# Moving the routing products of a recurrence from VectorE to GpSimd

## The chip, the cores and the metric

The kernel runs on one core of a Trainium2 chip. The metric is the device time of one execution, in microseconds (us), as the median of several runs. The engines are TensorE (PE in the profile, PEld for its weight loads), VectorE (DVE), ScalarE (ACT), GpSimd (POOL) and SyncE (SP), each with its own queue of instructions that it works off in order; they meet at semaphores.

## The reference, cut to what matters

The kernel computes a windowed attention block and then a mixture of experts, whose routing comes from a GRU. Only the GRU and the dot products made from its states matter here:

```python
xw = hidden_states @ gru_w_ih.T                  # per token, 3 * 1024 columns
def step(h, xw_t):                               # 512 steps, one after the other, batch 8
    hw = h @ gru_w_hh.T
    r = sigmoid(xr + hr); z = sigmoid(xz + hz); n = tanh(xn + r * hnn)
    h_new = (1.0 - z) * n + z * h
routing = l2norm(hs.reshape(B, S, 8, 128))       # eight vectors of 128 per token
expr = (hidden_states @ expr_w.T).reshape(B, S, 8, 128)
gram = einsum('bsed,bsfd->bsef', routing, routing)
num = sum(expr * routing); norm(expr); norm(routing)
```

The routing therefore needs, for each token and each of the eight experts e, products of length 128: the state of e with the states of e to e+4 (the Gram matrix is symmetric, so five shifts are enough), and the expression vector of e with the state and with itself.

## The kernel before, in words

The recurrence runs 512 steps in 32 tiles of 16 steps. A tile is 128 tokens (16 steps by batch 8), and its body is eight pairs of steps; the first pair of a tile is written out apart, the other seven are a loop. The steps of a pair are q = 0 and q = 1. Each step has two halves of the state, A (half 0) and B (half 1).

The cycle of one step is this. TensorE waits for `h_ready` of half B, does the last 32 matmuls that half A of the next step needs (L868), and signals `gates_psA`; it then does 48 more for half B (`gates_psB`), and 48 further matmuls that need only half A of the new state. VectorE turns the sums out of PSUM (L946, L947), adds their parts (L928), and with ScalarE's sigmoid (L1012) and tanh (L1015) and GpSimd's `keep` and `not_z` (L855, L856) makes the new half of the state: `fresh` (L968), the first fp16 part (L970), the fp32 state (L971), and the second fp16 part (L973), which signals `h_ready`. It does so for half A, then for half B.

Behind half B VectorE has work that belongs to the routing of the tile before, whose states ScalarE has copied into `routes` in the first pair of the present tile (L733, L736; `tile_read`). Pair i treats expert i:

- in step q = 0: the five state products, 128x640 (L746), and their sums along 128 (L751) into `gram`;
- in step q = 1: the turn of the next tokens' share (L934, L937), then the two expression products, 128x256 (L742), and their sums (L751).

Products and sums share one buffer, `products`. All of it is in program order on VectorE: the turn of half A of the next step (L946) stands behind the sums. `dots_half` and `dots_done` say that a pair's first and second sums are made.

Of the kernel before, what the change touches and what calls it, by code (L numbers as in the profile page):

```python
# [18 lines left out]
def sandwich(nc, x, qkv_w, qkv_b, rpb, proj_w, proj_b, w_ih, w_hh, expr_w, ctx_w, ctx_b,  # L19
# [27 lines left out]
    with ctx:  # L47
# [634 lines left out]
        x_tile = sb("x_tile", [P, P])  # L682
        routes = sb("routes", [P, 2, WRAP, P])
        products = sb("products", [P, NSHIFT, P])
        gram = sb("gram", [P, NT + 1, NEXP, NSHIFT + 2])
        xn_ps = sem("xn_ps")
        xn_read = sem("xn_read")
# [19 lines left out]
        tile_ps = sem("tile_ps")  # L707
        tile_read = sem("tile_read")
        tile_staged = sem("tile_staged")
        multiplied = sem("multiplied")  # L710
        dots_half = sem("dots_half")
        dots_done = sem("dots_done")

# [22 lines left out]
                last = nc.scalar.copy(routes[:, 1, 4 * h:4 * h + 4, :].rearrange("p e d -> p (e d)"), psum[:, 6 + h, :])  # L736
            return last

        def expr_dots(e):

            here = routes[:, :, bass.ds(e, 1), :].rearrange("p a e d -> p a (e d)")
            return nc.vector.tensor_tensor(products[:, 0:2, :], here, routes[:, 1, bass.ds(e, 1), :].to_broadcast([P, 2, P]), ALU.mult)  # L742

        def state_dots(e):

            return nc.vector.tensor_tensor(products[:, :, :], routes[:, 0, bass.ds(e, 1), :].to_broadcast([P, NSHIFT, P]),  # L746
                                           routes[:, 0, bass.ds(e, NSHIFT), :], ALU.mult)

        def sum_dots(slot, e, lo, n):
            dst = gram[:, bass.ds(slot, 1), bass.ds(e, 1), lo:lo + n].rearrange("p a e s -> p (a e s)")  # L750
            return nc.vector.tensor_reduce(dst, products[:, 0:n, :], axis=AX_X, op=ALU.add)  # L751

        def tokens(i):

# [5 lines left out]
        with nc.Block() as block:  # L760
# [17 lines left out]
            @block.vector  # L778
            def _(dve):
                nc.vector.tensor_reduce(x_mean[:, :], xn2T[:, :].rearrange("p (t b) -> p b t", b=B), axis=AX_X, op=ALU.add)  # L780
                dve.drain()
                nc.vector.tensor_scalar(x_mean[:, :], x_mean[:, :], 1.0 / L, None, ALU.mult).then_inc(mean_done, 1)
                dve.wait_ge(h0_ps, 1)
                dve.wait_ge(cleared, 1)
                full = by_chunk(h_full[:, 0, :])
                nc.vector.tensor_tensor(full, by_chunk(psum[:, 0, 0:CH * B]),
                                        ctx_bias[:, :].unsqueeze(2).to_broadcast([P, CH, B]), ALU.add)
                dve.drain()
                nc.vector.tensor_reduce(w_top[:, :], h_full[:, 0, :], axis=AX_X, op=ALU.max,
                                        apply_absolute_value=True).then_inc(h0_top, 1)  # L790


                dve.wait_ge(h0_all, 1)
                nc.vector.tensor_scalar(h_all[:, :], h_all[:, :], 1.0, None, ALU.max)
                dve.drain()
                nc.vector.tensor_scalar(h_exp[:, :], h_all[:, :].bitcast(U32), 0x7F800000, None, ALU.bitwise_and)
                dve.drain()
                nc.vector.tensor_scalar(h_scale[:, :], h_exp[:, :], -1.0, float(266 << 23), ALU.mult, ALU.add)
                nc.vector.tensor_scalar(h_unscale[:, :], h_exp[:, :], float(12 << 23), None, ALU.subtract)
                dve.drain().then_inc(h_scaled, 1)  # L800
                nc.vector.tensor_scalar(neg_h_scale[:, :], h_scale_f, -1.0, None, ALU.mult)
                nc.vector.tensor_tensor(unscale[:, :], w_unscale[:, :].bitcast(F32), h_unscale_f, ALU.mult)
                nc.vector.tensor_scalar(h_full[:, 0, :], h_full[:, 0, :], h_scale_f[:, 0:1], None, ALU.mult)
                dve.drain()
                nc.vector.tensor_copy(part(h_parts[:, 0, :, :], 0), full)
                dve.drain()
                nc.vector.tensor_tensor(part(h_parts[:, 0, :, :], 1), full, part(h_parts[:, 0, :, :], 0), ALU.subtract)
                for i in range(4):

                    dve.wait_ge(x_first, i + 1)  # L810
                    nc.vector.scalar_tensor_tensor(token_part(i, 1), tokens(i), h_scale_f[:, 0:1], token_part(i, 0),
                                                   ALU.mult, ALU.subtract)
                dve.drain()


                for half in range(2):
                    dve.sem_inc(h_ready[half], 1)
                    dve.sem_inc(bank_free[half], 1)
                dve.sem_inc(kept, 2)
                dve.sem_inc(tile_staged, 1)  # L820
                dve.sem_inc(tile_read, 1)
                dve.sem_inc(dots_done, 1)

            @block.tensor
# [6 lines left out]
        with nc.Block() as block:  # L831
# [12 lines left out]
            def _(pool):  # L844
                nc.gpsimd.tensor_copy(x_now[:, :], x_parts[:, 0:2, :].rearrange("p t k -> p (t k)")).then_inc(x_staged, 1)

                def pair(n, i, first):
# [4 lines left out]
                    for q in range(2):  # L852
                        for half in range(2):
                            pool.wait_ge(rz_done[half], t0 + q + 1)
                            nc.gpsimd.tensor_tensor(keep[:, half, :], rz[:, half, 1, :], h_full[:, q, half * HB:(half + 1) * HB], ALU.mult)  # L855
                            nc.gpsimd.tensor_scalar(not_z[:, half, :], rz[:, half, 1, :], neg_h_scale[:, 0:1], h_scale_f[:, 0:1], ALU.mult, ALU.add).then_inc(keep_done[half], 1)  # L856
                    if first:
                        nc.gpsimd.tensor_copy(x_tile[:, :], xn2T[:, bass.ds(n * P, P)]).then_inc(tile_staged, 1)

# [64 lines left out]
            def _(dve):  # L924
# [50 lines left out]
                def pair(n, i, first):  # L975
                    t0 = n * SP_T + 2 * i
                    for q in range(2):
# [7 lines left out]


                        if q == 0:
                            dve.wait_ge(tile_read, n + 2)
                            state_dots(i).then_inc(multiplied, 1)
                            dve.wait_ge(multiplied, t0 + 1)  # L990
                            sum_dots(n, i, 0, NSHIFT).then_inc(dots_half, 1)
                        else:
                            turn_xn(n * PAIRS + i + 2)
                            dve.wait_ge(dots_half, n * PAIRS + i + 1)
                            expr_dots(i).then_inc(multiplied, 1)
                            dve.wait_ge(xn_ready, n * PAIRS + i + 2)
                            dve.wait_ge(multiplied, t0 + 2)
                            sum_dots(n, i, NSHIFT, 2).then_inc(dots_done, 1)

                turn_xn(1)  # L1000
                dve.wait_ge(xn_ready, 1)
# [3 lines left out]
            def _(act):  # L1005
                def pair(n, i, first):
                    t0 = n * SP_T + 2 * i
                    for q in range(2):
                        t1 = t0 + q + 1
                        for half in range(2):  # L1010
# [10 lines left out]
                                       h_parts[:, 1 - q, :, 2 * (1 - q) * B:2 * (2 - q) * B].rearrange("p c (s b) -> p c s b", b=B)  # L1021
                                       ).then_inc(kept, 1)
                        if first and q == 0:
                            act.wait_ge(dots_done, n * PAIRS + 1)
                            tile_copies(act).then_inc(tile_read, 1)

# [18 lines left out]
        with nc.Block() as block:  # L1045
# [35 lines left out]
            def _(dve):  # L1081
                dve.wait_ge(last_read, 1)
                for e in range(NEXP):
                    expr_dots(e)
                    dve.drain()
                    sum_dots(NT, e, NSHIFT, 2)
                    dve.drain()
                    state_dots(e)
                    dve.drain()
                    sum_dots(NT, e, 0, NSHIFT)  # L1090
                    dve.drain()


# [316 lines left out]
```

## Time and profile before

| what | value |
|---|---|
| median of 3 runs | 4774.18 us (4764.96 to 4792.71) |
| span of the profiled execution | 4784.5 us (no other time of that execution is given) |
| TensorE busy | 3953.2 us, 83% |
| VectorE busy | 3284.3 us, 69% |
| ScalarE busy | 1204.3 us, 25% |
| GpSimd busy | 768.7 us, 16% |
| mean granted TensorE clock | 0.97 |

The recurrence fills the span from about 580 to 4330 us. Busy shares are means over the span; what sets the time of a step is read from the order of events inside one pair. A row of the timeline gives the start, the duration, the engine, the line, what is written and read, and in square brackets how long the engine was idle just before and what ended that.

### The profile page before, as it was taken

What the parts mean: (1) busy time and instruction counts of PE and PEld (TensorE: products, weight loads), DVE (VectorE), ACT (ScalarE), POOL (GpSimd) and SP (SyncE); (2) the same over time, 40 slices, a digit from 0 to 9 for tenths busy, and PEclk for the clock granted to TensorE, in tenths of its full rate; (3) what the DMA queues carried; (4) which work ended last, traced back from release to release, by engine and by line L of the source; (5) the groups of instructions that cost most, each with busy time, mean ns of one, the idle gap of its engine ahead of it and who ended that gap; (6) DMA issues with size and microseconds to landing.
All of it is one profiled execution on the core that took longest, in us unless ns stands there. A gap on an engine that the chain in (4) does not pass through costs nothing. (4 is left out here: it accounts for less than half of the span.)

```text
span 4784.5 us, 185112 instructions
## 1 busy us (share of the span) xinstructions
PE 3953.2 (83%) x76430; PEld 2476.3 (52%) x76430; DVE 3284.3 (69%) x13296; ACT 1204.3 (25%) x3094; POOL 768.7 (16%) x2439
## 2 busy tenths in 40 slices
PE   4998488888888888888888888888888888885999
PEld 3776354555544545544545545555554555453665
DVE  2668577777777777777777777777777777776555
ACT  1111322222222222222222222222222222222232
POOL 1111011111111111111111111111111111110000
PEclk9869799999999999999999999999999999997999
DMA  2001300000000000000000000000000000001000
GB/s 59 18 31 57 111 0 0 0 0 0 0 0 0 0 0 0 0 0 0 0 0 0 0 0 0 0 0 0 0 0 0 0 0 0 0 0 32 9 13 11
DMA packets 45745, 40.85 MB, mean 9 GB/s; under 512 B 11668, under 2 KB 39572, under 8 KB 45716
## 3 DMA queue, kind: packets, MB, share of 16 engines
q1 hardware_dynamic: 45716, 40.48, 2.7%
q8 instruction: 16, 0.26, 0.0%
q14 instruction: 13, 0.11, 0.0%
HBM read 36.28 MB, written 4.19 MB: 8 GB/s over the span
## 5 line engine op out<-in xcount | busy, mean ns | idle before, releaser
L868 PE MATMUL psum<-room,h_parts 128*32 128x384 f16 x65536 | 2904.9, 328 | 595.1 <-DVE h_parts L973 595.1
L868 PEld LDWEIGHTS psum<-room,h_parts 128*32 128x32 f16 x65536 | 1670.9, 97 | 1695.4 <-DVE h_parts L973 912.2
L1012 ACT ACTIVATE rz<-gates,unscale 128x64 f32<-128x64 f32 x1024 | 356.3, 348 | 1830.3 <-DVE gates L928 1830.3
L855 POOL TENSOR_TENSOR keep<-rz,h_full 128x32 f32<-128x32 f32 x1024 | 262.3, 256 | 2991.5 <-ACT rz L1012 2984.8
L946 DVE STREAM_TRANSPOSE turned<-psum 128x256 f32<-128x256 f32 x1024 | 454.1, 443 | 51.8 <-PE psum L868 16.9
L968 DVE TENSOR_TENSOR fresh<-n_act,not_z 128x32 f32<-128x32 f32 x1024 | 196.6, 192 | 401.7 <-ACT n_act L1015 397.4
L1015 ACT ACTIVATE n_act<-pre_n,unscale 128x32 f32<-128x32 f32 x1024 | 329.5, 322 | 497.4 <-DVE pre_n L959 497.4
L957 DVE TENSOR_TENSOR pre_n<-rz,gates 128x32 f32<-128x32 f32 x1024 | 197.2, 193 | 301.8 <-ACT rz L1012 301.8
L751 DVE TENSOR_REDUCE gram<-products 128x640 f32 (+3 forms) x528 | 327.6, 620 | 109.2 <-DVE products L742 53.8
L856 POOL TENSOR_SCALAR not_z<-rz,neg_h_scale,h_scale 128x32 f32<-128x32 f32 x1024 | 375.1, 366 | 0.0
L876 PE MATMUL psum<-w_ih_s,x_now 128*32 128x256 f16 x6152 | 305.1, 275 | 44.9 <-DVE turned L947 35.7
L928 DVE TENSOR_TENSOR gates<-turned 128x64 f32<-128x64 f32 (+1 forms) x2048 | 309.6, 187 | 0.0
L1291 PE MATMUL psum<-xn2T,room 128*128 x576 | 262.0, 600 | 38.8 <-DVE room L1366 31.4
L746 DVE TENSOR_TENSOR products<-routes 128x640 f32 (+1 forms) x264 | 218.0, 826 | 101.2 <-ACT routes L736 100.6
L947 DVE STREAM_TRANSPOSE turned<-psum 128x128 f32<-128x128 f32 x1024 | 280.1, 274 | 0.0
L1020 ACT COPY history<-h_parts 128x128 f16 (+1 forms) x512 | 152.6, 298 | 459.8 <-DVE h_parts L973 459.8
L876 PEld LDWEIGHTS psum<-w_ih_s,x_now 128*32 128x32 f16 x6152 | 160.0, 98 | 162.1 <-DVE turned L947 48.1
L959 DVE TENSOR_TENSOR pre_n<-pre_n,xn_pair 128x32 f32<-128x32 f32 x1024 | 196.7, 192 | 34.9
L973 DVE TENSOR_TENSOR h_parts<-h_full,h_parts 128x32 f16<-128x32 f32 x1024 | 196.2, 192 | 35.6
L970 DVE TENSOR_TENSOR h_parts<-fresh,keep 128x32 f16<-128x32 f32 x1024 | 196.5, 192 | 34.9
L1366 DVE TENSOR_TENSOR room<-room,psum 128x512 f32<-128x512 f32 x144 | 98.1, 686 | 142.9 <-ACT room L1308 140.9
L971 DVE TENSOR_TENSOR h_full<-fresh,keep 128x32 f32<-128x32 f32 x1024 | 188.4, 184 | 0.0
(151 smaller groups left out, 2725.6 us busy)
## 6 DMA issues: line engine op xcount, KB each, us to landing
xs_room<-in_L_ffn_gru_w_hh_dram SPq DMA_DIRECT2D x16, 1536.0 KB, 6.2
room<-in_L_attn_x_dram SPq DMA_DIRECT2D x8, 256.0 KB, 5.4
x_scratch<-room SPq DMA_DIRECT2D x8, 256.0 KB, 2.3
room<-x_scratch SPq DMA_DIRECT2D x32, 64.0 KB, 2.2
out_dram<-room SPq DMA_DIRECT2D x32, 64.0 KB, 2.0
xs_room<-in_L_ffn_gru_w_ih_dram SPq DMA_DIRECT2D x3, 512.0 KB, 5.1
xs_room<-in_L_ffn_gate_w_dram SPq DMA_DIRECT2D x2, 512.0 KB, 4.6
xs_room<-in_L_ffn_up_w_dram SPq DMA_DIRECT2D x2, 512.0 KB, 3.9
```

The costliest lines, as they stand in the source:

```text
L746: return nc.vector.tensor_tensor(products[:, :, :], routes[:, 0, bass.ds(e, 1), :].to_broadcast([P, NSHIFT, P]), routes[:, 0, bass.ds(e, N ...
L751: return nc.vector.tensor_reduce(dst, products[:, 0:n, :], axis=AX_X, op=ALU.add)
L855: nc.gpsimd.tensor_tensor(keep[:, half, :], rz[:, half, 1, :], h_full[:, q, half * HB:(half + 1) * HB], ALU.mult)
L856: nc.gpsimd.tensor_scalar(not_z[:, half, :], rz[:, half, 1, :], neg_h_scale[:, 0:1], h_scale_f[:, 0:1], ALU.mult, ALU.add).then_inc(keep_d ...
L868: last = nc.tensor.matmul(psum[32 * j:32 * j + 32, half, 0:3 * P], h_parts[:, q, c, :], w_hh_s[:, s, half, 4 * c + j, :, :].rearrange("p g ...
L876: last = nc.tensor.matmul(psum[32 * j:32 * j + 32, columns, 0:2 * P], x_now[:, :], w_ih_s[:, s, j, place:place + 2, :].rearrange("p g r -> ...
L928: return nc.vector.tensor_tensor(by_chunk(gates[:, half, g:g + n, :].rearrange("p g k -> p (g k)")), by_part[:, :, 2 * q, :], by_part[:, : ...
L946: nc.vector.transpose(turned[:, half, 0:2, :], bank[:, 0:2, :]).then_inc(rz_turned[half], 1)
L947: nc.vector.transpose(turned[:, half, 2:3, :], bank[:, 2:3, :]).then_inc(bank_free[half], 1)
L1012: nc.scalar.activation(rz[:, half, :, :], gates[:, half, 0:2, :], ACT.Sigmoid, scale=unscale[:, 0:1]).then_inc(rz_done[half], 1)
L1015: nc.scalar.activation(n_act[:, half, :], pre_n[:, half, 1, :], ACT.Tanh, scale=unscale[:, 0:1]).then_inc(n_done[half], 1)
L1291: last = nc.tensor.matmul(psum[:, 2 * (u % RING) + k, :], expT[:, e, FC * k + f, :], toks, start=True, stop=True)
```

## The change

The two sets of products are computed by GpSimd, both in step q = 0 behind its `keep` and `not_z` of half B, the expression products first, into a buffer of their own (`expr_prod`), then the state products into `products`. VectorE only sums: the expression products in step q = 0, the state products in step q = 1. The semaphore `multiplied` gives way to `expr_multiplied` and `state_multiplied`, and GpSimd waits for `dots_half` and `dots_done` before it writes a buffer again. In the block after the recurrence the last tile's products stay on VectorE, with fewer drains.

```diff
+        expr_prod = sb("expr_prod", [P, 2, P])
...
+                        if q == 0:
+
+                            pool.wait_ge(tile_read, n + 2)
+                            pool.wait_ge(dots_half, n * PAIRS + i + 1)
+                            expr_dots(nc.gpsimd, i).then_inc(expr_multiplied, 1)
+                            pool.wait_ge(cleared, 1)
+                            pool.wait_ge(dots_done, n * PAIRS + i + 1)
+                            state_dots(nc.gpsimd, i).then_inc(state_multiplied, 1)
...
                         if q == 0:
-                            dve.wait_ge(tile_read, n + 2)
-                            state_dots(i).then_inc(multiplied, 1)
-                            dve.wait_ge(multiplied, t0 + 1)
-                            sum_dots(n, i, 0, NSHIFT).then_inc(dots_half, 1)
+                            dve.wait_ge(expr_multiplied, n * PAIRS + i + 1)
+                            sum_dots(n, i, NSHIFT, 2, expr_prod).then_inc(dots_half, 1)
                         else:
                             turn_xn(n * PAIRS + i + 2)
-                            dve.wait_ge(dots_half, n * PAIRS + i + 1)
-                            expr_dots(i).then_inc(multiplied, 1)
                             dve.wait_ge(xn_ready, n * PAIRS + i + 2)
-                            dve.wait_ge(multiplied, t0 + 2)
-                            sum_dots(n, i, NSHIFT, 2).then_inc(dots_done, 1)
+                            dve.wait_ge(state_multiplied, n * PAIRS + i + 1)
+                            sum_dots(n, i, 0, NSHIFT, products).then_inc(dots_done, 1)
...
                         if first and q == 0:
+                            act.wait_ge(dots_half, n * PAIRS + 1)
                             act.wait_ge(dots_done, n * PAIRS + 1)
...
-                    expr_dots(e)
+                    expr_dots(nc.vector, e)
+                    state_dots(nc.vector, e)
                     dve.drain()
-                    sum_dots(NT, e, NSHIFT, 2)
-                    dve.drain()
-                    state_dots(e)
-                    dve.drain()
-                    sum_dots(NT, e, 0, NSHIFT)
+                    sum_dots(NT, e, NSHIFT, 2, expr_prod)
+                    sum_dots(NT, e, 0, NSHIFT, products)
                     dve.drain()
```

GpSimd's queue, in the body of a pair of the inner loop, in the kernel before (both steps; L855 is `keep`, L856 `not_z`, the first two rows are half A of step q = 0):

```order
L855 TENSOR_TENSOR keep<-rz,h_full 128x32 [waits rz_doneA]
L856 TENSOR_SCALAR not_z<-rz,neg_h_scale,h_scale 128x32
L855 TENSOR_TENSOR keep<-rz,h_full 128x32 [waits rz_doneB]
L856 TENSOR_SCALAR not_z<-rz,neg_h_scale,h_scale 128x32
L855 TENSOR_TENSOR keep<-rz,h_full 128x32 [waits rz_doneA]
```

The same place in the changed kernel, whose lines L858 and L859 are `keep` and `not_z`:

```order
L858 TENSOR_TENSOR keep<-rz,h_full 128x32 [waits rz_doneA]
L859 TENSOR_SCALAR not_z<-rz,neg_h_scale,h_scale 128x32
L858 TENSOR_TENSOR keep<-rz,h_full 128x32 [waits rz_doneB]
L859 TENSOR_SCALAR not_z<-rz,neg_h_scale,h_scale 128x32
L744 ISA [waits dots_half,tile_read]
L744 TENSOR_TENSOR expr_prod<-routes 128x256
L748 TENSOR_TENSOR products<-routes 128x640 [waits dots_done,cleared]
L858 TENSOR_TENSOR keep<-rz,h_full 128x32 [waits rz_doneA]
```

Two products have moved in between `not_z` of half B in step q = 0 and `keep` of half A in step q = 1.

VectorE's queue in the kernel before, from the last operations of half B in step q = 0 to the turn of half A in step q = 1:

```order
L968 TENSOR_TENSOR fresh<-n_act,not_z 128x32 [waits keep_doneB,n_doneB]
L970 TENSOR_TENSOR h_parts<-fresh,keep 128x4x8 [waits fresh_doneB]
L971 TENSOR_TENSOR h_full<-fresh,keep 128x32
L973 TENSOR_TENSOR h_parts<-h_full,h_parts 128x4x8 [waits first_partB]
L746 ISA [waits tile_read]
L746 TENSOR_TENSOR products<-routes 128x640
L751 ISA [waits multiplied]
L751 TENSOR_REDUCE gram<-products 128x5
L946 STREAM_TRANSPOSE turned<-psum 128x256 [waits kept,gates_psA]
```

The same place in the changed kernel (L979, L981, L982 and L984 are `fresh`, the first part, the fp32 state and the second part; L957 is the turn):

```order
L979 TENSOR_TENSOR fresh<-n_act,not_z 128x32 [waits keep_doneB,n_doneB]
L981 TENSOR_TENSOR h_parts<-fresh,keep 128x4x8 [waits fresh_doneB]
L982 TENSOR_TENSOR h_full<-fresh,keep 128x32
L984 TENSOR_TENSOR h_parts<-h_full,h_parts 128x4x8 [waits first_partB]
L999 ISA
L753 ISA [waits expr_multiplied]
L753 TENSOR_REDUCE gram<-expr_prod 128x2
L957 STREAM_TRANSPOSE turned<-psum 128x256 [waits kept,gates_psA]
```

A product of 640 and a sum of 640 have given way to a sum of 256 that waits for GpSimd.

At the end of step q = 1 the changed kernel has this; before, L742 (products, 128x256) stood between L937 and the sum, and the sum was that of 256:

```order
L945 STREAM_TRANSPOSE xn_turned<-psum 128x256 [waits xn_ps]
L948 TENSOR_TENSOR xn_pair<-xn_turned 128x128 [waits xn_read]
L753 ISA [waits state_multiplied,xn_ready]
L753 TENSOR_REDUCE gram<-products 128x5
L843 REGISTER_ALU
L843 COMPARE_AND_BRANCH
```

The product has gone from VectorE here, and the sum behind it has grown from 256 to 640.

## Rows read from the trace of the kernel before

**Rows 1.** Busy time by engine over the recurrence; the first number is the stretch

```profile
580.00:4345.00 3765.00, 3123.47 (x72209) 1880.86 (x72208) 2684.70 (x11780) 970.21 (x2761) 686.74 (x2335) 0.99 0.00 1
```

**Rows 2.** Timeline, end of step q = 0 of an inner pair

```profile
2007.75 0.36 POOL L856 TENSOR_SCALAR not_z<-rz,neg_h_scale,h_scale 128x32 f32<-128x32 f32 x1
...
2008.26 0.19 DVE L968 TENSOR_TENSOR fresh<-n_act,not_z 128x32 f32<-128x32 f32 x1 [0.39 <-ACT n_act L1015]
2008.48 0.19 DVE L970 TENSOR_TENSOR h_parts<-fresh,keep 128x32 f16<-128x32 f32 x1
...
2008.81 0.19 DVE L973 TENSOR_TENSOR h_parts<-h_full,h_parts 128x32 f16<-128x32 f32 x1
...
2009.06 3.44 PE L868 MATMUL psum<-room,h_parts 128*32 128x384 f16 x80 [0.50 <-DVE h_parts L973]
...
2009.98 0.82 DVE L751 TENSOR_REDUCE gram<-products 128x640 f32 x1 [0.22 <-DVE products L746]
2010.71 0.44 DVE L946 STREAM_TRANSPOSE turned<-psum 128x256 f32<-128x256 f32 x1
```

**Rows 3.** Timeline, 32 matmuls of the same kind in one run

```profile
2013.48 1.48 PE L868 MATMUL psum<-room,h_parts 128*32 128x384 f16 x32 [0.77 <-DVE h_parts L973]
```

**Rows 4.** Timeline, step q = 1 of the tile's first pair, from the inner loop's entry

```profile
2002.11 3.43 PE L868 MATMUL psum<-room,h_parts 128*32 128x384 f16 x80 [0.28 <-DVE h_parts L973]
...
2003.65 0.45 DVE L946 STREAM_TRANSPOSE turned<-psum 128x256 f32<-128x256 f32 x1
```

**Rows 5.** Timeline, end of step q = 1 of an inner pair

```profile
2015.86 0.19 DVE L973 TENSOR_TENSOR h_parts<-h_full,h_parts 128x32 f16<-128x32 f32 x1
...
2016.11 3.43 PE L868 MATMUL psum<-room,h_parts 128*32 128x384 f16 x80 [0.28 <-DVE h_parts L973]
2016.46 0.29 DVE L937 TENSOR_TENSOR xn_pair<-xn_turned 128x128 f32<-128x128 f32 x1
...
2017.30 0.42 DVE L751 TENSOR_REDUCE gram<-products 128x256 f32 x1 [0.21 <-DVE products L742]
2017.87 0.45 DVE L946 STREAM_TRANSPOSE turned<-psum 128x256 f32<-128x256 f32 x1
```

**Rows 6.** Timeline, VectorE at the end of a tile's last pair

```profile
2103.28 0.45 DVE L946 STREAM_TRANSPOSE turned<-psum 128x256 f32<-128x256 f32 x1 [0.32 <-issue]
```

**Rows 7.** Timeline, step q = 0 of a tile's first pair, where routes are copied

```profile
1993.90 1.08 ACT L736 COPY routes<-psum 128x512 f32<-128x512 f32 x2
...
1996.72 0.44 DVE L946 STREAM_TRANSPOSE turned<-psum 128x256 f32<-128x256 f32 x1
...
1997.28 0.30 DVE L928 TENSOR_TENSOR gates<-turned 128x64 f32<-128x64 f32 x2
```

**Rows 8.** Timeline of GpSimd alone: not_z and the next instruction in its queue

```profile
2000.80 0.37 POOL L856 TENSOR_SCALAR not_z<-rz,neg_h_scale,h_scale 128x32 f32<-128x32 f32 x1
...
2001.11 0.28 POOL L858 COPY x_tile<-xn2T 128x128 f32 x1
```

**Rows 9.** Attention stage, VectorE's products alone (L338, both inputs in SBUF)

```profile
61.32 0.68 DVE L338 TENSOR_TENSOR room<-room 128x500 f32<-128x500 f32 x1 [7.53 <-ACT room L453]
171.88 0.17 DVE L338 TENSOR_TENSOR room<-room 128x12 f32<-128x12 f32 x1
```

**Rows 10.** Attention stage, the same product behind a GpSimd product (L437)

```profile
207.39 1.07 POOL L437 TENSOR_TENSOR room<-room 128x500 f32<-128x500 f32 x1 [33.65 <-ACT room L453]
207.53 1.47 DVE L338 TENSOR_TENSOR room<-room 128x500 f32<-128x500 f32 x1
61.91 1.04 DVE L338 TENSOR_TENSOR room<-room 128x12 f32<-128x12 f32 x1
```

**Rows 11.** Attention stage, GpSimd products one behind the other, and VectorE behind them

```profile
210.57 0.21 POOL L437 TENSOR_TENSOR room<-room 128x12 f32<-128x12 f32 x1
210.74 1.24 POOL L437 TENSOR_TENSOR room<-room 128x500 f32<-128x500 f32 x1
211.22 1.29 DVE L338 TENSOR_TENSOR room<-room 128x500 f32<-128x500 f32 x1
```

More of the change, by code:

```diff
@@ L709, in sandwich @@
         tile_staged = sem("tile_staged")
-        multiplied = sem("multiplied")
+        expr_multiplied = sem("expr_multiplied")
+        state_multiplied = sem("state_multiplied")
         dots_half = sem("dots_half")
@@ L737, in tile_copies, with expr_dots, state_dots, sum_dots @@
             return last
-        def expr_dots(e):
+        def expr_dots(eng, e):
             here = routes[:, :, bass.ds(e, 1), :].rearrange("p a e d -> p a (e d)")
[L742 to L749, printed above, removed]
+            return eng.tensor_tensor(expr_prod[:, :, :], here, routes[:, 1, bass.ds(e, 1), :].to_broadcast([P, 2, P]), ALU.mult)
+        def state_dots(eng, e):
+            return eng.tensor_tensor(products[:, :, :], routes[:, 0, bass.ds(e, 1), :].to_broadcast([P, NSHIFT, P]),
+                                     routes[:, 0, bass.ds(e, NSHIFT), :], ALU.mult)
+        def sum_dots(slot, e, lo, n, of):
             dst = gram[:, bass.ds(slot, 1), bass.ds(e, 1), lo:lo + n].rearrange("p a e s -> p (a e s)")
-            return nc.vector.tensor_reduce(dst, products[:, 0:n, :], axis=AX_X, op=ALU.add)
+            return nc.vector.tensor_reduce(dst, of[:, :, :], axis=AX_X, op=ALU.add)
         def tokens(i):
@@ L821, in _ @@
                 dve.sem_inc(tile_read, 1)
+                dve.sem_inc(dots_half, 1)
                 dve.sem_inc(dots_done, 1)
```

## The prediction

> **What bounds the kernel now.** I read the page first: no engine is full, and TensorE has 83%. Over the recurrence [rows 1] TensorE is busy 3123 of 3765 us and VectorE 2685, at a granted clock of 0.99 (the upper of its two levels, 2.4 GHz). A loop with two engines at 83% and 71% is bound by what they hand each other, so the timeline of one inner pair comes next. The cycle is: VectorE finishes half B (L973), TensorE starts 0.25 us behind L973's start, does 32 matmuls, and VectorE turns half A (L946). At the end of step q = 0 [rows 2] TensorE starts at 2009.06; 32 such matmuls take 1.48 us [rows 3], so half A is ready at 2010.54. VectorE's sum ends at 9.98 + 0.82 = 10.80 and the turn starts at 10.71, 0.17 us behind the data. That the turn can start 0.06 behind it is seen at the inner loop's entry [rows 4]: 2002.11 + 1.48 = 3.59 against 3.65. At the end of step q = 1 [rows 5] the data is there at 2016.11 + 1.48 = 17.59, the sum ends at 17.72, and the turn starts at 17.87, 0.28 behind the data, since the loop's branch stands between. So both engines arrive almost together. **However much work leaves VectorE behind L973, a step can give back 0.11 us in q = 0 and 0.22 in q = 1, no more.** The rest of VectorE's path (L946 to L973, twice a step) is bound by itself and untouched.
>
> **The change, part by part.** A tile has eight pairs, seven of them in the inner loop; there are 32 tiles.
>
> *Step q = 0, VectorE.* 0.83 us of products and 0.82 of sums go; a sum of 256 (0.42, as in [rows 5]) comes. It is over at about 2009.5 if GpSimd is in time, and the turn then starts 0.06 behind the data: -0.11 us in each of seven pairs.
>
> *Step q = 1, VectorE.* The product of 256 goes, but the sum becomes the one of 640. L937 ends at 2016.75; the sum follows 0.21 later (the idle time that stands before it now), 16.96 to 17.78. The turn starts some 0.08 before a sum of this size ends, as in [rows 2]: 17.70 instead of 17.87, -0.17 us. The branch is hidden under the longer sum. That is for six pairs. Behind a tile's first pair the turn was already at its floor and now waits for the longer sum: +0.06. Behind its last pair the 0.32 us of issue [rows 6] go under the sum: about -0.30.
>
> *GpSimd's queue.* The products stand behind `not_z` of half B. `not_z` starts at 2007.75 [rows 2], and the next instruction in this queue starts 0.31 us after it [rows 8]: the expression product starts at 2008.06, with its semaphores long met. What a GpSimd product costs is seen in the attention stage. A 12-column one starts 0.17 us before its neighbour [rows 11]. One of 500 lasts 1.07 [rows 10] or 1.24 [rows 11], and durations stand 0.03 above the spacing: 1.04 or 1.21. That is (1.04 - 0.17) / 488 = 1.78 ns or 2.13 ns a column, so 0.60 or 0.69 us for 256 columns and 1.29 or 1.51 for 640. Both fit before `keep` of the next step is asked for, over 3 us later. By queue length alone the move is free.
>
> *What the products do to VectorE.* This is the term that decides. L338 takes two inputs from SBUF. Alone, its 500-column form takes 0.68 us and its 12-column form 0.17 [rows 9]. Issued at 207.53, behind a GpSimd product that started at 207.39, it lasts 1.47; a 12-column one behind another GpSimd product lasts 1.04 [rows 10]. Taking 0.67 off its end, the first began its work at 208.33, which is 0.94 after GpSimd's start, or 0.10 before that product's spacing is over. With the slower product [rows 11]: 211.22 + 1.29 - 0.67 = 211.84, 1.10 after 210.74. So VectorE does not run slower beside such a product; it stands still until GpSimd has read its inputs, small as its own instruction may be. By SBUF — State Buffer, section "Who interferes with whom", of the Trainium skill, a VectorE instruction with two SBUF inputs and a GpSimd instruction that reads SBUF exclude each other for a whole instruction; the trace agrees.
>
> L968, L970 and L971 have two SBUF inputs each, and the new products run just there. With the slower rate: the expression product from 2008.06 frees the inputs at 8.06 + 0.59 = 8.65; L968, due at 8.26, does its work then, 0.39 late, and L970 would be issued 0.22 behind, at 8.87. But the state product starts at 8.06 + 0.69 = 8.75, before it, and holds the inputs until 8.75 + 1.41 = 10.16. L970, due at 8.48, goes then: **1.68 us late**, and with it L973, TensorE, and the next step. Nothing covers this: TensorE is already idle before that point. With the faster rate: 8.06 + 0.60 = 8.66, + 1.19 = 9.85, and the delay is 1.37.
>
> Which rate? In [rows 11] (the slower) both inputs start at the same offset of their tiles, in the first of [rows 10] they are six columns apart; `routes` is read at whole multiples of 128 columns, which is nearer to the slower. I take 2.13 ns. GPSIMD Engine Reference, "Performance versus the Vector engine", of the Trainium skill gives 4497 ns for 2048 columns, so 1.41 us for 640 by proportion; by that page the state product holds the inputs about as long as my sum has it.
>
> *First pair of a tile.* VectorE waits there for the copies of `routes`, done at 1993.90 + 1.08 = 1994.98 [rows 7], and then needs until 1996.72 for product and sum. Now: expression product from 1995.03 to 5.72, 0.21 of wake-up, sum of 0.42, turn at 6.26, so -0.46. The state product holds inputs from 5.72 to 7.13; L928, whose inputs are both in SBUF, is due at 1997.28 - 0.46 = 6.82 and waits 0.31. Net -0.15 (faster rate: -0.55 + 0.09 = -0.46).
>
> *The rest.* ScalarE's extra wait is for something older than what it already waits for. The block after the recurrence loses two drains for each of eight experts, beside TensorE's and ScalarE's work on the weights: nothing.
>
> **Sum.** A tile: 7 x (1.68 - 0.11) = 10.99; -6 x 0.17 = -1.02; +0.06; -0.30; -0.15; together +9.58 us, times 32 is +307 us. The profiled span of 4784.5 becomes 5091; that span is 0.2% over the median of the runs, 4774, so the median becomes **5081 us**. With the faster rate a tile is 8.82 - 1.02 + 0.06 - 0.30 - 0.46 = +7.10, +227, 5001 us.
>
> **The rivals.** A measurement of this kernel tells about 0.5% (24 us) from no change.
>
> *No standing still (faster).* If small VectorE instructions slip in beside GpSimd's, only the gains are left: -0.77 - 1.02 + 0.06 - 0.30 - 0.55 = -2.58 a tile, -83 us, 4691. For it: `keep` and `not_z` already run beside L957 and L959 and nobody is seen to wait; but these are short, and start after VectorE's. Against it: the 12-column instruction of [rows 10] lost 0.87 us. 0.06.
>
> *Only the first product hits (about no change).* If the state product reached SBUF after L970, L971 and L973, only L968's 0.39 would remain (0.30 by the faster rate): 7 x (0.39 - 0.11) = 1.96, with the other terms +0.55 a tile, +18 us, 4792; by the faster rate -12, some 4762. It needs the state product to start over 0.4 us later than the spacing of GpSimd's products says. The point at which all gains are eaten is 0.31 us of delay in a pair. 0.04.
>
> *GpSimd becomes late itself.* `keep` of the next step would have to wait for the state product. That ends near 2010.3, and `keep` is wanted after 2013 by then. It would need the products to be twice as dear; 0.02, slower than my forecast.
>
> The forecast, standing still through both products, has 0.88: 0.50 with the slower rate, 0.38 with the faster or between.
>
> **How the numbers follow.** The range reaches from 4975 (the faster rate with L970 getting in ahead of the state product and L971 behind it, which saves 0.1 to 0.2 us a pair, some 25 us) to 5110 (the slower rate, and 0.13 us more a pair of wake-ups): about 8 in 10. Faster by over 0.5%: 0.06. Within: 0.04. Slower: 0.90.
>
> **What would show it.** In the changed kernel's trace, in step q = 0 alone: L979 (`fresh`) of half B lasts 0.5 to 0.6 us instead of 0.19, L981 (the first part) 1.3 to 1.5, L982 and L984 their old 0.19; in step q = 1 and for half A all are as before. TensorE's idle time before its 80 matmuls grows from 0.50 to about 2.2 us in q = 0 and stays 0.28 in q = 1. The turn starts 0.06 behind the data in q = 0, and about 0.1 in q = 1. GpSimd's products last about 0.7 and 1.5 us. I am wrong if L981 keeps its 0.19, if the state product starts behind L984, or if the granted clock falls below 0.99 in the recurrence with TensorE's longer idle time, which would add to every matmul.

## The result, and the profile after

The changed kernel takes 5129.28 us (median of 4 runs, 5107.12 to 5174.16) against 4770.83 before; the ratio is 1.0743 (95% interval 1.0685 to 1.0800). The profiled execution took 5107.12 us with a span of 5105.4 us, at a mean granted clock of 0.95 (0.97 before). It is the shortest of the four: the others, at 0.946, 0.946 and 0.935, took 5126, 5133 and 5174 us.

The timeline of one inner pair of the changed kernel, step q = 0, answers to [rows 2]:

```profile
2104.27 0.36 POOL L859 TENSOR_SCALAR not_z<-rz,neg_h_scale,h_scale 128x32 f32<-128x32 f32 x1
...
2104.60 0.67 POOL L744 TENSOR_TENSOR expr_prod<-routes 128x256 f32 x1
2104.78 0.54 DVE L979 TENSOR_TENSOR fresh<-n_act,not_z 128x32 f32<-128x32 f32 x1 [0.39 <-ACT n_act L1022]
2105.23 1.47 POOL L748 TENSOR_TENSOR products<-routes 128x640 f32 x1
2105.35 1.40 DVE L981 TENSOR_TENSOR h_parts<-fresh,keep 128x32 f16<-128x32 f32 x1
2106.67 0.18 DVE L982 TENSOR_TENSOR h_full<-fresh,keep 128x32 f32<-128x32 f32 x1
2106.88 0.19 DVE L984 TENSOR_TENSOR h_parts<-h_full,h_parts 128x32 f16<-128x32 f32 x1
...
2107.13 3.43 PE L879 MATMUL psum<-room,h_parts 128*32 128x384 f16 x80 [2.05 <-DVE h_parts L984]
...
2107.20 0.42 DVE L753 TENSOR_REDUCE gram<-expr_prod 128x256 f32 x1
2108.66 0.45 DVE L957 STREAM_TRANSPOSE turned<-psum 128x256 f32<-128x256 f32 x1 [1.04 <-PE psum L879]
```

VectorE's L979 lasts 0.54 us and L981 lasts 1.40 us, each 0.19 before. Taking 0.19 off their ends, L979 began its work at 2105.13, when the expression product was nearly through, and L981 at 2106.56, when the state product was. Without a stall L981 would have run at 2104.78 + 0.22 = 2105.00, so half B is 1.56 us late. TensorE's idle time in front of its 80 matmuls has grown from 0.50 to 2.05 us, and VectorE then waits for TensorE (1.04 us): here it has time to spare. The end of step q = 1 answers to [rows 5]:

```profile
2114.08 3.43 PE L879 MATMUL psum<-room,h_parts 128*32 128x384 f16 x80 [0.28 <-DVE h_parts L984]
...
2114.42 0.29 DVE L948 TENSOR_TENSOR xn_pair<-xn_turned 128x128 f32<-128x128 f32 x1
2114.85 0.82 DVE L753 TENSOR_REDUCE gram<-products 128x640 f32 x1
2115.62 0.45 DVE L957 STREAM_TRANSPOSE turned<-psum 128x256 f32<-128x256 f32 x1
```

The turn is 0.06 us behind the data (2114.08 + 1.48 = 15.56), at its floor. The pair from turn to turn (L957 at 2100.17, the next pair's at 2115.62) takes 15.45 us; before it was 14.20 us (median of 192 inner pairs).

That is 1.25 us for 7 pairs in 32 tiles, 280 us, less what a tile's ends give back. The rest of the loss is in other rows of the same trace. One pair later (15.45 us) TensorE's same 80 matmuls:

```profile
2122.58 5.12 PE L879 MATMUL psum<-room,h_parts 128*32 128x384 f16 x80 [2.05 <-DVE h_parts L984]
...
2125.36 0.45 DVE L957 STREAM_TRANSPOSE turned<-psum 128x256 f32<-128x256 f32 x1 [2.29 <-PE psum L879]
```

They take 5.12 us instead of 3.43, and VectorE waits 2.29 us, instead of 1.04, for the first 32 of them. The windows view of that stretch, with the granted clock behind the engines, and below it the same view of the whole recurrence:

```profile
2122.60:2126.00 3.40, 3.40 (x44) 1.82 (x48) 1.06 (x4) 0.30 (x1) 0.00 (x0) 0.51 0.00 0
...
533.45:4651.29 4117.84, 3265.93 (x72224) 1948.68 (x72216) 2767.63 (x11251) 964.12 (x2748) 1217.89 (x2845) 0.96 0.00 0
```

The clock was at its lower level (1.2 GHz) in this stretch. In the changed kernel's recurrence the clock's records hold 107 such stretches, 365 us in all; in the kernel before, 11 and 38 us. From the first turn to the last the recurrence takes 4117.8 us against 3749.1.

### The profile page after: what moved, and what is told of

Its sections match the earlier page's. It is cut to its first block and busy times, and to the rows that moved or that the text cites. A ratio compares the mean times of both kernels' runs of the same rounds, so it can differ in the third digit from the quotient of the medians.

```text
span 5105.4 us, 185417 instructions
## 1 busy us (share of the span) xinstructions
PE 4055.3 (79%) x76430; PEld 2507.2 (49%) x76430; DVE 3374.0 (66%) x12784; ACT 1204.5 (24%) x3094; POOL 1300.4 (25%) x2951
## 5 line engine op out<-in xcount | busy, mean ns | idle before, releaser
L879 PE MATMUL psum<-room,h_parts 128*32 128x384 f16 x65536 | 3066.2, 341 | 843.1 <-DVE h_parts L984 842.7
L879 PEld LDWEIGHTS psum<-room,h_parts 128*32 128x32 f16 x65536 | 1743.0, 101 | 2020.1 <-DVE h_parts L984 1141.5
L858 POOL TENSOR_TENSOR keep<-rz,h_full 128x32 f32<-128x32 f32 x1024 | 264.5, 258 | 2709.9 <-ACT rz L1019 2702.6
L957 DVE STREAM_TRANSPOSE turned<-psum 128x256 f32<-128x256 f32 x1024 | 457.7, 447 | 346.8 <-PE psum L879 345.6
L979 DVE TENSOR_TENSOR fresh<-n_act,not_z 128x32 f32<-128x32 f32 x1024 | 276.4, 270 | 401.3 <-ACT n_act L1022 397.3
L981 DVE TENSOR_TENSOR h_parts<-fresh,keep 128x32 f16<-128x32 f32 x1024 | 466.8, 456 | 35.0
L748 POOL TENSOR_TENSOR products<-routes 128x640 f32 (+1 forms) x256 | 376.5, 1471 | 0.0
L859 POOL TENSOR_SCALAR not_z<-rz,neg_h_scale,h_scale 128x32 f32<-128x32 f32 x1024 | 375.3, 367 | 0.0
L753 DVE TENSOR_REDUCE gram<-products 128x640 f32 (+1 forms) x264 | 216.5, 820 | 34.7
L984 DVE TENSOR_TENSOR h_parts<-h_full,h_parts 128x32 f16<-128x32 f32 x1024 | 196.4, 192 | 35.5
L753 DVE TENSOR_REDUCE gram<-expr_prod 128x256 f32 (+1 forms) x264 | 111.0, 421 | 156.4 <-POOL expr_prod L744 128.7
L744 POOL TENSOR_TENSOR expr_prod<-routes 128x256 f32 (+1 forms) x256 | 170.6, 667 | 130.6 <-ACT routes L738 130.6
```

What stands on the lines that cost most here:

```text
L748: return eng.tensor_tensor(products[:, :, :], routes[:, 0, bass.ds(e, 1), :].to_broadcast([P, NSHIFT, P]), routes[:, 0, bass.ds(e, NSHIFT) ...
L753: return nc.vector.tensor_reduce(dst, of[:, :, :], axis=AX_X, op=ALU.add)
L879: last = nc.tensor.matmul(psum[32 * j:32 * j + 32, half, 0:3 * P], h_parts[:, q, c, :], w_hh_s[:, s, half, 4 * c + j, :, :].rearrange("p g ...
L957: nc.vector.transpose(turned[:, half, 0:2, :], bank[:, 0:2, :]).then_inc(rz_turned[half], 1)
L981: nc.vector.tensor_tensor(part(parts, 2 * (1 - q)), by_chunk(fresh[:, half, :]), by_chunk(keep[:, half, :]), ALU.add)
```

## The experiments

All times are medians beside runs of the kernel before on the same chip (4773.5 us for e1 to e4, 4770.9 for e5 to e8, 4768.2 for e9 and e10). A "pair" is the time from turn to turn of an inner pair at the full clock, "falls" are the stretches at half the clock in the recurrence.

| kernel | median, us | ratio to before (95%) | pair, us | falls |
|---|---|---|---|---|
| before | 4770.8 | 1 | 14.20 | 11 |
| the change | 5129.3 | 1.0743 (1.0685 to 1.0800) | 15.45 | 107 |
| e1_behind_half_b | 4707.9 | 0.9867 (0.9818 to 0.9915) | 14.05 | 23 |
| e2_write_only | 4693.9 | 0.9835 (0.9787 to 0.9883) | 13.90 | 19 |
| e3_own_stall | 5214.4 | 1.0919 (1.0846 to 1.0991) | 15.69 | 63 |
| e4_filled | 5491.7 | 1.1499 (1.1443 to 1.1555) | 16.84 | 95 |
| e5_filled_q1 | 5023.5 | 1.0516 (1.0480 to 1.0552) | 15.45 | 1 |
| e6_expr_only | 4826.8 | 1.0097 (1.0061 to 1.0134) | 14.34 | 23 |
| e7_behind_state | 4691.8 | 0.9837 (0.9807 to 0.9868) | 13.89 | 20 |
| e8_behind_half_b_again | 4702.3 | 0.9860 (0.9830 to 0.9890) | 14.02 | 27 |
| e9_filled_tile | 4663.5 | 0.9779 (0.9751 to 0.9807) | 13.90 | 0 |
| e10_behind_state_again | 4697.1 | 0.9834 (0.9807 to 0.9862) | 13.90 | 24 |

**The same work at another moment.**

```diff
                             pool.wait_ge(tile_read, n + 2)
+                            pool.wait_ge(h_ready[1], t0 + 2)
                             pool.wait_ge(dots_half, n * PAIRS + i + 1)
                             expr_dots(nc.gpsimd, i).then_inc(expr_multiplied, 1)
```

> The changed kernel with one wait more: GpSimd starts the products of a pair only when half B of step q = 0 is finished (h_ready of half B), so that they run while VectorE has a sum with one SBUF input, a wait and transposes out of PSUM before it. Theory (a GpSimd instruction that reads SBUF holds up VectorE instructions with two SBUF inputs): L979 and L981 are back at 0.19 us, an inner pair takes 13.9 us instead of 15.45 (14.20 before the change), TensorE's clock stays up, and the median is 4690 to 4720, faster than the kernel before. Rival (GpSimd is simply too late with its products, or its load as such slows the loop): the products come 0.9 us later than in the changed kernel, so the time is no better than 5130.

One wait more turned a loss of 7.4% into a gain of 1.3%. Its timeline at the same place (L980, L982, L983, L985 are `fresh` to the second part, L940 the sum of half A's parts in the next step):

```profile
2113.35 0.19 DVE L980 TENSOR_TENSOR fresh<-n_act,not_z 128x32 f32<-128x32 f32 x1 [0.39 <-ACT n_act L1023]
2113.58 0.19 DVE L982 TENSOR_TENSOR h_parts<-fresh,keep 128x32 f16<-128x32 f32 x1
...
2113.91 0.19 DVE L985 TENSOR_TENSOR h_parts<-h_full,h_parts 128x32 f16<-128x32 f32 x1
2114.15 3.43 PE L880 MATMUL psum<-room,h_parts 128*32 128x384 f16 x80 [0.50 <-DVE h_parts L985]
...
2114.36 0.67 POOL L744 TENSOR_TENSOR expr_prod<-routes 128x256 f32 x1 [1.16 <-issue]
2114.99 1.49 POOL L748 TENSOR_TENSOR products<-routes 128x640 f32 x1
2115.28 0.42 DVE L753 TENSOR_REDUCE gram<-expr_prod 128x256 f32 x1 [1.18 <-POOL expr_prod L744]
2115.69 0.45 DVE L958 STREAM_TRANSPOSE turned<-psum 128x256 f32<-128x256 f32 x1
2116.26 0.41 DVE L940 TENSOR_TENSOR gates<-turned 128x64 f32<-128x64 f32 x2
```

The products run at the length that they have in the changed kernel beside a sum with one input and a transpose out of PSUM, and neither is stretched (0.42, 0.45). Only their tail touches L940, two instructions in 0.41 us instead of 0.30; that is why the pair is 14.05 us and not the 13.9 expected. So the rival, that GpSimd is too late or too loaded, is out: its products come later here and the kernel is faster than before the change.

**GpSimd busy, but not reading.**

```diff
+        written = sb("written", [P, 1500], F16)
...
-                            expr_dots(nc.gpsimd, i).then_inc(expr_multiplied, 1)
-                            pool.wait_ge(cleared, 1)
                             pool.wait_ge(dots_done, n * PAIRS + i + 1)
-                            state_dots(nc.gpsimd, i).then_inc(state_multiplied, 1)
+                            nc.gpsimd.tensor_tensor(expr_prod[:, 0, 0:32], x_tile[:, 0:32], x_tile[:, 0:32], ALU.mult)
+                            nc.gpsimd.memset(expr_prod[:, 0, 32:128], 0.0)
+                            nc.gpsimd.memset(expr_prod[:, 1, :], 0.0)
+                            nc.gpsimd.memset(written[:, 0:250], 0.0).then_inc(expr_multiplied, 1)
+                            nc.gpsimd.memset(products[:, :, :], 0.0)
+                            nc.gpsimd.memset(written[:, 250:1250], 0.0).then_inc(state_multiplied, 1)
```

> The changed kernel with GpSimd's two products replaced, at the same place of its queue, by a 32-column product and by memsets of about the same total length, which write SBUF and read nothing (the dot products are left out: VectorE sums zeros and old values). Theory (it is GpSimd's reading that holds VectorE up): L981 lasts its 0.19 us, L979 at most 0.3, an inner pair takes some 13.9 us, the median is about 4700. Rival (any GpSimd instruction there, writing ones too, shuts VectorE out): L979 and L981 together last over 1.3 us more and the median stays above 5000.

Its timeline, at the place where the changed kernel stands still (L983, L985, L986, L988 are `fresh` to the second part):

```profile
2106.41 0.23 POOL L866 TENSOR_TENSOR expr_prod<-x_tile 128x32 f32<-128x32 f32 x1
2106.59 0.17 POOL L867 MEMSET expr_prod<- 128x96 f32 x1
2106.59 0.19 DVE L983 TENSOR_TENSOR fresh<-n_act,not_z 128x32 f32<-128x32 f32 x1 [0.39 <-ACT n_act L1026]
2106.70 0.20 POOL L868 MEMSET expr_prod<- 128x128 f32 x1
2106.82 0.19 DVE L985 TENSOR_TENSOR h_parts<-fresh,keep 128x32 f16<-128x32 f32 x1
2106.85 0.30 POOL L869 MEMSET written<- 128x250 f16 x1
2106.93 0.19 DVE L986 TENSOR_TENSOR h_full<-fresh,keep 128x32 f32<-128x32 f32 x1
2107.10 0.63 POOL L870 MEMSET products<- 128x640 f32 x1
2107.15 0.19 DVE L988 TENSOR_TENSOR h_parts<-h_full,h_parts 128x32 f16<-128x32 f32 x1
```

This kernel leaves the dot products out. GpSimd's short product ends as `fresh` begins, then GpSimd only writes, beside all four VectorE instructions, and none is stretched; the pair is 13.90 us. What holds VectorE up is the part of GpSimd's product that a `memset` does not have: its reading of SBUF. The Trainium skill says so of these pairs of instructions (SBUF — State Buffer, "Who interferes with whom": against a VectorE instruction with two SBUF inputs, a GpSimd instruction contends only if it reads); the run agrees.

**One product alone.** In this kernel GpSimd makes only the expression product, at its place of the change; L976, L978 are `fresh` and the first part.

```diff
                             pool.wait_ge(tile_read, n + 2)
-                            pool.wait_ge(dots_half, n * PAIRS + i + 1)
+                            pool.wait_ge(dots_done, n * PAIRS + i + 1)
                             expr_dots(nc.gpsimd, i).then_inc(expr_multiplied, 1)
-                            pool.wait_ge(cleared, 1)
-                            pool.wait_ge(dots_done, n * PAIRS + i + 1)
-                            state_dots(nc.gpsimd, i).then_inc(state_multiplied, 1)
...
-                            dve.wait_ge(expr_multiplied, n * PAIRS + i + 1)
-                            sum_dots(n, i, NSHIFT, 2, expr_prod).then_inc(dots_half, 1)
+                            dve.wait_ge(tile_read, n + 2)
+                            state_dots(nc.vector, i).then_inc(state_multiplied, 1)
+                            dve.wait_ge(state_multiplied, n * PAIRS + i + 1)
+                            sum_dots(n, i, 0, NSHIFT, products).then_inc(dots_half, 1)
...
-                            dve.wait_ge(state_multiplied, n * PAIRS + i + 1)
-                            sum_dots(n, i, 0, NSHIFT, products).then_inc(dots_done, 1)
+                            dve.wait_ge(expr_multiplied, n * PAIRS + i + 1)
+                            sum_dots(n, i, NSHIFT, 2, expr_prod).then_inc(dots_done, 1)
```

> Only the expression product (256 columns) on GpSimd, at its place of the changed kernel; the state product stays on VectorE in step q = 0, and the expression sum stands in q = 1 as before the change. Theory (each product that GpSimd reads holds up the VectorE instruction behind it): L979 lasts 0.54 us and the first part its 0.19, so an inner pair is 14.20 + 0.35 in q = 0 and - 0.20 in q = 1, about 14.35 us, and the median 4800 to 4830. Rival (the delay comes with GpSimd's being busy as such, in proportion to both products): also the first part is late, and the pair is over 14.6 us.

```profile
2103.49 0.67 POOL L744 TENSOR_TENSOR expr_prod<-routes 128x256 f32 x1
2103.67 0.54 DVE L976 TENSOR_TENSOR fresh<-n_act,not_z 128x32 f32<-128x32 f32 x1 [0.39 <-ACT n_act L1021]
2104.24 0.19 DVE L978 TENSOR_TENSOR h_parts<-fresh,keep 128x32 f16<-128x32 f32 x1
```

`fresh` is stretched by 0.35 us as in the changed kernel, the first part is not; the pair is 14.34 us against the expected 14.35. Each product stops the one VectorE instruction that comes up while it reads, and the two delays do not add: in the change the first part can go only when the state product has read, and its 1.56 us hold the 0.35 of `fresh`.

**The clock: a stall without GpSimd.** To the kernel before:

```diff
+        idle_sum = sb("idle_sum", [P, 1])
+        idle_sum2 = sb("idle_sum2", [P, 1])
...
+                    if q == 0 and half == 1:
+                        nc.vector.tensor_reduce(idle_sum[:, :], exprT[:, :], axis=AX_X, op=ALU.add)
+                        nc.vector.tensor_reduce(idle_sum2[:, :], exprT[:, 0:256], axis=AX_X, op=ALU.add)
                     nc.vector.tensor_tensor(part(parts, 2 * (1 - q)), by_chunk(fresh[:, half, :]), by_chunk(keep[:, half, :]), ALU.add)
```

> The kernel before with a stall of VectorE's own making at the place where the changed one stands still: two sums over constant data (1024 and 256 columns) between fresh and the first part of half B in step q = 0 of every pair; GpSimd has no new work. The stall is about 1.48 us a pair, 379 us in all. Theory (TensorE's longer idle time in each pair makes its granted clock fall for short stretches): some 100 stretches at half the clock in the recurrence instead of 11, and some 70 us on top: 5190 to 5250. Rival (the clock has nothing to do with TensorE's idle time but with GpSimd's load, or was chance): about 11 stretches and 5150.

```profile
2101.86 3.43 PE L870 MATMUL psum<-room,h_parts 128*32 128x384 f16 x80 [1.96 <-DVE h_parts L978]
```

The stall is 15.69 - 14.20 = 1.49 us a pair, 381 us over 256 pairs; the recurrence is 449 us longer, so 68 us are left beside the stall, where I had expected 70. TensorE's idle time of 1.96 us brought 63 falls with no new work for GpSimd, where I had expected some 100; together they are 266 us at half the clock (365 in the change). GpSimd's load is therefore not needed for the falls; why this kernel has 63 and the change, with 2.05 us, 107, stays open.

**The clock: filling TensorE's idle time.** To the changed kernel, first at the wrong place (`q == 0`), then at the right one:

```diff
                         state_share(q, 1, range(0, EARLY))
+                        if q == 1:
+                            for k in range(10):
+                                nc.tensor.matmul(psum[:, 3, 0:3 * P], ident_16[:, :],
+                                                 w_hh_s[:, 0, 0, k, :, :].rearrange("p g r -> p (g r)"),
+                                                 start=True, stop=True)
                         pe.wait_ge(h_ready[1], t1)
```

> The changed kernel with ten matmuls of 384 columns on constant weights into an unused PSUM bank, in step q = 0 ahead of TensorE's wait for half B, so that its idle time of 2.05 us there is filled for some 1.6 us. Theory (idle TensorE lets the clock fall): the stretches at half the clock go from 107 in the recurrence to about 10, an inner pair stays at 15.45 us, and the median falls by some 60 to 85 us to 5045 to 5070. Rival (the falls come from something else): as many stretches as in the changed kernel and 5130 or more.

Neither theory had 5492 us. TensorE's q = 0 waits for VectorE's q = 1, where it was idle for 0.28 us only, so the ten matmuls of 1.8 us stood in the way of every pair (+1.39 us). The miss has its use. TensorE had more to do than in the changed kernel (82% busy in the recurrence against 79%), and its idle time ahead of the other 80 matmuls was untouched:

```profile
2098.17 3.43 PE L879 MATMUL psum<-room,h_parts 128*32 128x384 f16 x80 [2.05 <-DVE h_parts L989]
...
566.20:5041.31 4475.11, 3678.14 (x74774) 2154.13 (x74766) 2775.36 (x11252) 969.33 (x2748) 1219.33 (x2845) 0.96 0.00 0
```

The second row is the windows view of its recurrence. The clock fell 95 times, where about 10 were expected.

> The changed kernel with the ten idle matmuls ahead of the wait that TensorE really stands in for 2.05 us. In e4_filled they stood in TensorE's q = 0, whose wait is for half B of the step before, that is for VectorE's q = 1, where only 0.28 us were idle; now they stand in TensorE's q = 1. Theory (a long idle time of TensorE in a pair lets its clock fall): the stretches at half the clock fall from 107 to under 30, an inner pair stays at 15.45 us and the median is 5045 to 5070. Rival (TensorE's idle time doesn't matter, a busier TensorE even brings more falls): 100 stretches or more and 5130 or above.

In the timeline of e5_filled_q1 the ten matmuls (L924) stand in the gap, and VectorE's stall is what it was (L986 is the first part):

```profile
2107.29 1.80 PE L924 MATMUL psum<-room,ident 128*128 128x384 f16 x10
...
2107.62 1.41 DVE L986 TENSOR_TENSOR h_parts<-fresh,keep 128x32 f16<-128x32 f32 x1
...
2109.41 3.43 PE L879 MATMUL psum<-room,h_parts 128*32 128x384 f16 x80 [0.32 <-DVE h_parts L989]
```

Its windows view over the recurrence:

```profile
578.37:4585.92 4007.55, 3543.36 (x74784) 2097.87 (x74776) 2752.58 (x11252) 964.92 (x2748) 1221.32 (x2845) 1.00 0.00 0
```

One fall instead of 107, the granted clock 1.00 instead of 0.96, the pair unchanged, the recurrence 110 us shorter and the median 106 us lower, more than the 60 to 85 us expected. Work whose result nobody uses has bought 2% by keeping TensorE from being idle.

**A better place, and the clock again.** e7_behind_state is e1_behind_half_b with another semaphore:

```diff
-                            pool.wait_ge(h_ready[1], t0 + 2)
+                            pool.wait_ge(first_part[1], t0 + 1)
```

> As e1_behind_half_b, but GpSimd starts one instruction earlier: it waits for the fp32 state of half B (first_part), as the second fp16 part on VectorE does. Theory: GpSimd wakes 0.05 us behind VectorE from the same semaphore, as keep does behind L957, so the second part keeps its 0.19 us, the products end some 0.2 us earlier than in e1_behind_half_b, the 0.13 us that the sum of half A's parts (L940 there) lost behind the state product are gone, an inner pair takes 13.90 us instead of 14.05 and the median is 20 to 40 us below e1_behind_half_b. Rival (GpSimd gets in first): the second part lasts 0.7 us, the pair is 14.4 us or more, and the median is above e1_behind_half_b.

> The kernel e1_behind_half_b once more, beside e7_behind_state on the same chip: both theories expect 4690 to 4720 and an inner pair of 14.05 us.

```profile
2116.37 0.19 DVE L985 TENSOR_TENSOR h_parts<-h_full,h_parts 128x32 f16<-128x32 f32 x1
2116.60 0.67 POOL L744 TENSOR_TENSOR expr_prod<-routes 128x256 f32 x1 [0.94 <-issue]
2117.22 1.49 POOL L748 TENSOR_TENSOR products<-routes 128x640 f32 x1
...
2118.72 0.30 DVE L940 TENSOR_TENSOR gates<-turned 128x64 f32<-128x64 f32 x2
```

The pair is 13.89 us against 14.02 beside it, L940 is back at 0.30, and the ratio 0.9837 against 0.9860. The pair came true. The median lies only 10.5 us below its neighbour's (20 to 40 expected) and the intervals overlap, though the profiled recurrence is 36 us shorter (3676.3 against 3712.4). My reason did not come true: GpSimd did not wake 0.05 us behind VectorE but 0.23 us behind the start of L985, 0.22 earlier than in e1_behind_half_b against its own L985. So the two did not meet for the inputs at all.

e9_filled_tile is e7_behind_state with the ten matmuls once a tile, behind TensorE's work for the first pair (`if first:` after the loop over q).

> e7_behind_state with the ten idle matmuls once a tile, behind TensorE's work of the tile's first pair, where it is idle for 1.96 us and where, in 20 of 32 tiles, the next 32 matmuls then took 2.55 us instead of 1.48. Theory (this idle time lets the clock fall): no fall there, the turn behind the tile's first pair comes 4.31 us after its neighbour in every tile instead of 5.48 in most, 20 times 1.17 us are won, the recurrence takes about 3653 us instead of 3676, and the median is 15 to 30 us below e7_behind_state. Rival (the fall follows from the products of the tile, whatever TensorE does after them): as many falls, and the same time as e7_behind_state or a few us more.

> The kernel e7_behind_state once more, beside e9_filled_tile on the same chip: both theories expect some 4690 us and an inner pair of 13.89 us.

TensorE's rows in e7_behind_state (first) and in e9_filled_tile (second fence), at the same place of a tile:

```profile
1932.50 0.40 PE L888 MATMUL psum<-w_ih_s,x_now 128*32 128x256 f16 x8 [0.20 <-DVE turned L959]
1934.86 2.55 PE L880 MATMUL psum<-room,h_parts 128*32 128x384 f16 x32 [1.96 <-DVE h_parts L985]
```

```profile
1921.58 1.80 PE L934 MATMUL psum<-room,ident 128*128 128x384 f16 x10
1923.31 0.40 PE L888 MATMUL psum<-w_ih_s,x_now 128*32 128x256 f16 x8
1924.22 1.48 PE L880 MATMUL psum<-room,h_parts 128*32 128x384 f16 x32 [0.51 <-DVE h_parts L990]
```

No fall is left in the recurrence, and the turn behind the first pair comes after 4.31 us in every tile (without the ten matmuls 20 of 32 took over 5 us). This kernel is the fastest: 4663.5 us, ratio 0.9779, 34 us under the same kernel without the matmuls beside it (15 to 30 expected). The 11 falls of the kernel before stand at this place too, behind the first pair of every third tile, where TensorE is idle for 1.67 us.

## Why the prediction was wrong

The mechanism, its place and its sign were right; the time, 5129 us, lies 48 us above the forecast of 5081 and 19 us above the range.

- **The stop of VectorE in step q = 0**: right in kind. L979 lasts 0.54 us (0.5 to 0.6 forecast), L981 1.40 (1.3 to 1.5), L982 and L984 are untouched. The delay is 1.56 us, not 1.68: GpSimd's products start 2105.23 - 2104.60 = 0.63 us apart, that is (0.63 - 0.17) / 244 = 1.89 ns a column, nearer to the rate that I did not take; the state product held the inputs for 2106.56 - 2105.23 = 1.33 us, between the 1.19 and the 1.41 of my two rates and nearer to the one that I took. The 0.12 us less are 0.12 x 7 x 32 = 27 us less than the sum has. TensorE's idle time is 2.05 us, 2.2 forecast.
- **The gains on VectorE**: 0.12 instead of 0.11 in q = 0 (the turn is 0.05 us behind the data, 0.17 before); 0.20 instead of 0.17 in q = 1 of the inner pairs (turn to turn 4.31 us after half B's, 4.51 before), 0.39 instead of 0.30 at a tile's end, and nothing instead of +0.06 behind its first pair, because the sum started 0.14 us behind L948's end and not 0.21. Some 11 us.
- **First pair of a tile**: the turn came 0.49 us earlier (0.46 forecast) and the next half 0.29 later (0.31). Right, to 0.05 us a tile, some 2 us.
- **The clock**: this is the step that failed. I took the time of 32 matmuls, 1.48 us, over from the kernel before for every step, and named a lower granted clock only as something that would make me wrong, with no price and no share in the range. It came: 0.96 in the recurrence. The change itself makes TensorE idle for 2.05 us in each pair, and with that its clock fell 107 times instead of 11. e5_filled_q1 prices it: its recurrence is 110 us shorter, and some 5 us more would be won if the added matmuls did not stand in the way of a tile's first pair (17.10 us there against 16.94 in the change; the turn comes 0.44 us later, but the next half meets the state product no more and wins 0.27 back). So the falls cost about 115 us. The kernel before loses 13 us to its own 11 (some 1.2 us each, 5.5 us instead of 4.31 behind the tile's first pair). The change has added about 102 us.
- **The balance**: the recurrence is 369 us longer (4117.8 - 3749.1). About 102 are the clock; the other 267 stand against 307 in my sum, which lost 27 at the delay, some 11 at the gains and 2 in the first pair. Without the clock the sum would have been too high, not too low: the two errors cancel in part, and it is luck that the median misses by only 48 us. Ahead of the recurrence the two profiled executions differ by 43 us the other way (the first turn stands at 576.5 us before and at 533.5 after); in the ten other profiled executions, whose work up to there is the same, it stands between 536 and 580, so that difference says nothing of the change. That early start is also why the profiled execution, at 5107 us, lies just inside the range.
- **The range**: it held the uncertainty of the stop, about 80 us, and nothing for the clock.
- **The rivals**: "no standing still" gave 4691 us, and e2_write_only and e7_behind_state, where VectorE does not stand still, came to 4694 and 4692. "Only the first product hits" was the first of two stops, and e6_expr_only shows it alone. GpSimd itself was never late.

## What to carry to other kernels

When work moves from VectorE to GpSimd, price what GpSimd's reads do to the VectorE instructions with two SBUF inputs that fall into their time, and put the reads beside sums, PSUM transposes or waits: here the same two products cost 7.4% where they start 0.2 us ahead of `fresh` (some 2% of it the clock), and gave 1.6% where they start 0.8 us behind it. When a change lengthens TensorE's idle time inside a loop, its clock is part of the price, and cheap matmuls nobody reads may pay, provided they stand in the gap and not in front of a wait that is short.

## What the runs showed of the hardware

- A VectorE instruction that was stopped by GpSimd's reading shows no idle time before it; it shows as a long duration (1.40 us for a 128x32 product). It is counted as busy: VectorE's busy time rose by 90 us in the page although 1.25 us of work a pair had left it (the products of 0.83 and 0.42 us).
- GpSimd's writing does not stop the same instructions: `memset`s of 96 to 640 columns beside them left them at 0.19 us.
- TensorE's clock fell in a loop in which TensorE was 79% busy (3265.93 of 4117.84 us) with one idle time of 2.05 us a pair, 107 times in 256 pairs; with the same loop and that idle time filled down to 0.32 us, once. With 82% busy (3678 of 4475 us in e4_filled) and the 2.05 us left open it fell 95 times. The kernel before, 83% busy with no idle time over 0.9 us in its inner pairs, had no fall there; its 11 stand behind the tiles' first pairs, at 1.67 us.
